# Later and closer-packed transposition of the embedding stages in a DLRM tower: stage schedule moved towards each stage's first use

## The reference

```python
e = jnp.stack([tbl_0[ids[:, 0]], ..., tbl_31[ids[:, 31]]], axis=1)    # (2048, 32, 64)
z = jnp.sum(e, axis=-1)                                               # (2048, 32)
outer = jnp.einsum('bpd,pde,bpe->bp', e[:, II], kernels, e[:, JJ])    # 496 pairs i < j
h = jnp.concatenate([z, outer, dense_ctx], axis=1)                    # 544 features
h = jnp.maximum(h @ W_top1 + b_top1, 0.0)                             # 512
h = jnp.maximum(h @ W_top2 + b_top2, 0.0)                             # 256
y = h @ W_top3                                                        # 1
```

## Time and profile before

| | |
|---|---|
| median of 3 runs | 1015.3 us (1012.37 to 1015.33) |
| the profiled execution's own time | 1018.13 us |
| its span, first to last instruction | 1016.3 us |
| PE busy | 886.5 us, 87% of the span |
| DVE busy | 641.3 us, 63% |
| POOL busy (issuing gathers) | 483.6 us, 48% |
| ACT busy | 69.3 us, 7% |
| DMA | 28.20 MB, mean 28 GB/s |

### The profile page before, as it was taken

The page is one execution under the profiler, slowest core; times in us unless marked ns, Lnnn a source line. Parts: engine busy times, 40 slices in busy tenths (PEclk is TensorE's granted clock), DMA queues, the critical chain, the costliest instruction groups (busy, mean ns, idle before and its releaser), DMA issues.

```text
span 1016.3 us, 11896 instructions
## 1 busy us (share of the span) xinstructions
PE 886.5 (87%) x4608; PEld 311.6 (31%) x4608; DVE 641.3 (63%) x579; ACT 69.3 (7%) x113; POOL 483.6 (48%) x518
## 2 busy tenths in 40 slices
PE   0323579699999999998999999998999999999998
PEld 0111123223333333333333333323333333333333
DVE  0102257578887575687877656676787657688850
ACT  0000000000000001000000101000000101000001
POOL 5774735536565444555666444554556445400000
PEclk9956779999999999999999999999999999999999
DMA  9310101101111000110111010011101000000000
GB/s 348 107 27 15 27 14 19 21 12 23 23 21 23 17 17 18 20 21 20 22 23 22 15 19 17 19 22 19 21 19 24 15 17 19 19 1 1 1 1 0
DMA packets 19777, 28.20 MB, mean 28 GB/s; under 512 B 8901, under 2 KB 9413, under 8 KB 18825
## 3 DMA queue, kind: packets, MB, share of 16 engines
q0 software_dynamic: 16384, 16.81, 8.6%
q1 hardware_dynamic: 3336, 10.63, 2.9%
HBM read 27.40 MB, written 0.01 MB: 27 GB/s over the span
## 4 chain that ended last, share of the span: by engine, by line
PE 77%; another core or an unknown queue 8%; issue 7%; DVE 4%; DMA 2%; ACT 1%; SPq 1%; POOL 1%; DVEq 0%; POOLq 0%
PE m_ps L386 39%; PE acc L398 21%; PE tr L341 4%; DVE prod L300 3%; PE tr L328 3%; PE tr L347 2%; PE m_ps L387 2%; DMA w_sb<-in_w 2%; PE m_ps L341 1%; PE tr L339 1%; PE m_ps L347 1%; PE tr L353 1%; POOL gathered L176 1%; SPq L186 1%
## 5 line engine op out<-in xcount | busy, mean ns | idle before, releaser
L300 DVE TENSOR_TENSOR prod<-m_ps,x_t 128x1024 f32<-128x1024 f32 x512 | 604.3, 1219 | 302.5 <-PE m_ps L387 180.7
L176 POOL DMA_INDIRECT gathered<-in_tbl,idx x512 | 482.9, 943 | 403.4 <-DVE prod L300 178.2
L386 PE MATMUL m_ps<-x_t,k_sb 64*128 64x512 f32 x1024 | 501.4, 623 | 74.6 <-DVE prod L300 35.6
L387 PE MATMUL m_ps<-x_t,k_sb 64*128 64x512 f32 x1024 | 502.3, 624 | 0.0
L386 PEld LDWEIGHTS m_ps<-x_t,k_sb 64*128 64x128 f32 x1024 | 180.7, 191 | 346.9 <-issue 261.6
L398 PE MATMUL acc<-prod,sel 128*32 128x512 f32 x2048 | 247.0, 600 | 0.0
L387 PEld LDWEIGHTS m_ps<-x_t,k_sb 64*128 64x128 f32 x1024 | 180.6, 191 | 0.0
L398 PEld LDWEIGHTS acc<-prod,sel 128*32 128x32 f32 x2048 | 53.7, 109 | 176.5 <-issue 119.6
L328 PE MATMUL tr<-ident,gathered 128*128 128x128 f32 x256 | 44.5, 299 | 50.6 <-DMA gathered<-in_tbl,idx 41.4
L213 ACT ACTIVATE x_t<-tr 128x512 f32<-128x512 f32 x64 | 38.2, 597 | 471.7 <-PE tr L328 275.3
L287 DVE TENSOR_REDUCE z_nat<-gathered 128x8 f32<-128x512 f32 x64 | 43.1, 675 | 38.1 <-DMA gathered<-in_tbl,idx 38.1
(11 more groups left out here) (24 smaller groups left out, 39.6 us busy)
## 6 DMA issues: line engine op xcount, KB each, us to landing
gathered<-in_tbl,idx POOLq DMA_INDIRECT x512
k_sb<-in_kmat SPq DMA_DIRECT2D x7, 1024.0 KB, 14.3
w_sb<-in_w SPq DMA_DIRECT2D x1, 1280.0 KB
k_sb<-in_kmat SPq DMA_DIRECT2D x2, 256.0 KB, 4.2
k_sb<-in_kmat SPq DMA_DIRECT2D x1, 512.0 KB, 6.4
w_sb<-in_w SPq DMA_DIRECT2D x1, 512.0 KB
idx<-in_ids SPq DMA_DIRECT2D x1, 256.0 KB, 2.7
z_sb<-in_dense_t SPq DMA_DIRECT2D x4, 32.0 KB
```

Of the source, the lines that this page charges most:

```text
L176: nc.gpsimd.indirect_dma_start(out=gathered[:, G % GR, t, f, :], out_offset=None, in_=tables[2 * (STAGES - 1 - a) + f], in_offset=bass.Ind ...
L300: nc.vector.tensor_tensor(prod[:, p % PR, :, :], m_ps[:, p % MR, :, :], other, ALU.mult).then_inc(prod_ready, 1)
L386: nc.tensor.matmul(m_ps[:, p % MR, 0, :], k_sb[0:D, d, :], x_t[0:D, q % 2, a0, :], start=True, stop=True)
L387: nc.tensor.matmul(m_ps[:, p % MR, 1, :], k_sb[D:P, d, :], x_t[D:P, q % 2, a1, :], start=True, stop=True).then_inc(unit_done, 1)
```

## The change

The table of places is redrawn and the gates move with it; no instruction is added or taken away. In quarter 0, stages 6, 7, 8 and 11 to 15 move back by 1, 1, 1, 2, 4, 5, 7 and 10 groups; stages up to 8 now stand directly ahead of the group that first uses them, later ones one group earlier. In a later quarter, stage 0 stands behind group 28 of the quarter before, stage 1 behind 30, and then stage a behind the group just ahead of its first use: 31, then 0, 1, 2, 3, 5, 7, 9, 11, 14, 17, 20, 23 of its own quarter, and 26 for stage 15. The entry "s" moves to group 28. The gates open four groups ahead of the transposition in place of three: they begin at group 24, 26, 27, 28, 29, 30, 31 of the quarter before and 1, 3, 5, 7, 10, 13, 16, 19, 22 of its own.

```diff
--- before.py
+++ after.py
@@ -61,11 +61,11 @@
 
 def group_of_stage(q, a):
 
-    return 18 + 32 * (q - 1) + 2 * a
+    return min(NG * q - 4 + 2 * a, NG * q + FIRST[a] // GROUP - 1)
 
 
 for _a in range(STAGES):
-    _g = 0 if _a < 3 else min(FIRST[_a] // GROUP - (_a > 5), (4 * _a - 7) // 3)
+    _g = FIRST[_a] // GROUP - (_a > 8)
     BEFORE.setdefault((0, _g), []).append(("x", 0, _a))
 for _q in range(1, NQ):
     for _n in range(H1 // P):
@@ -75,8 +75,8 @@
     AFTER.setdefault((_q, 13), []).append(("y", _q - 1, 0))
     for _a in range(STAGES):
         AFTER.setdefault(divmod(group_of_stage(_q, _a), NG), []).append(("x", _q, _a))
-    AFTER.setdefault((_q, 18), []).append(("s", _q, 0))
-AFTER.setdefault((0, NG - 1), []).append(("s", 0, 0))
+    AFTER.setdefault((_q, 28), []).append(("s", _q, 0))
+AFTER.setdefault((0, 28), []).insert(0, ("s", 0, 0))
 ORDER = [e for q in range(NQ) for g in range(NG) for e in BEFORE.get((q, g), []) + AFTER.get((q, g), [])]
 PLACE = {e: n for n, e in enumerate(ORDER)}
 
@@ -167,7 +167,7 @@
                     t, f = divmod(n, 2)
                     if q:
 
-                        pool.wait_ge(prod_ready, GROUP * (group_of_stage(q, a) - 3) + n)
+                        pool.wait_ge(prod_ready, GROUP * (group_of_stage(q, a) - 4) + n)
                     k = G * GATHERS + n
                     if k >= IN_FLIGHT:
```

## The result

The changed kernel takes 1140.94 us (median of 3 runs, 1137.72 to 1144.64) against 1015.3 us before: ratio 1.125, 95% interval 1.119 to 1.131. It is slower by an eighth. Its profiled execution has a span of 1139.1 us, 122.8 more than before.

The account below looks back on a forecast made before the run. PE mostly bounds the kernel, with gathers closer than about 1.5 us delaying TensorE's reports as second bound. Terms 87 - 28.2 + 3.6 - 8.3 - 8.1 + 23.2 + 16.0 + 0.9 = +86.1 us gave 1101 us, range 1035 to 1155.

Parts of the forecast that it names:

- the one with 0.50: Total time: the forecast's own band, 1070 to 1134 us, given chance 0.50.
- Term 1: Ends of quarters: packed gathers delay TensorE's signals, 29 us a boundary, +87 us for three (21 to 120).
- The price of the 15-run: Quarter 0 before the change: 15 unbroken gathers cost 10.9 us, 0.73 us each.
- the even groups of 10 + 1.8 us: Boundaries: the self-limiting run makes five groups take 10 + 1.8 us in place of 6.07, 29 us a boundary.
- Term 2: Same stretches lose their present excess, groups 8 to 24 getting fewer gathers: -28.2 us; stages 0 and 1 keep theirs, +3.6.
- Term 3: Quarter 0: the run of 16 gathers ends at 8, -8.3 us; the run of 15 goes, -8.1 us.
- Terms 4 and 5: PE waits for ScalarE's copies: just-before-use transpositions 29 x 0.80, +23.2 us; behind dense layers 18 x 0.89, +16.0; stage 0, +0.9.
- Term 6: Row sums moved on VectorE: free, since it idles at each group's end.
- Short price: Boundaries: 0.18 us per gather, 21 us in place of 87; 1035 us, band 1020 to 1070, chance 0.25.
- Heavy price: Boundaries: 1.0 us per gather, and late copies of stages 3 to 6 on PE's path; 1134 to 1194 us, chance 0.15.
- Faster: Boundaries: gates hold gathers to one per product, so boundaries cost nothing; 1011 us, chance 0.06.

Follow-up runs that it names:

- Experiment 12: The changed kernel with a GpSimd memset of 128x336 behind every gather, which puts gathers 1.51 us apart: 984.8 us, ratio 0.953.
- experiment 6: The kernel before, with only the gates of quarters 1 to 3 opened for 16 gathers of two stages at once: 1277.4 us, ratio 1.260.
- kernel 9: The kernel before with a GpSimd memset of 128x336 behind every gather, gathers 1.51 us apart: 969.2 us, ratio 0.935.
- Experiment 3: The changed kernel with stages 7 to 15 of quarters 1 to 3 transposed one group earlier, gates untouched: 1116.2 us, ratio 1.098.
- experiment 5: The changed kernel with a GpSimd memset of 128x256 behind every gather, gathers 1.44 us apart: 1053.6 us, ratio 1.039.
- experiment 1: The changed kernel with only the gates spread, opening at groups 18 to 54 counted from the quarter before: 1102.3 us, ratio 1.084.

## Why the prediction was right, and where its sizes were off

The forecast was 1101 us with a range of 1035 to 1155, and slower at 0.91; it came out at 1140.9. Mechanism and sign hold. The sum was 36.7 us short (86.1 against 122.8), by the table 15.7 of them at the boundaries, 9.5 ahead of the 28th reduction of quarter 0 and 11.7 between the boundaries; and the time lies in the band to which I gave 0.15, not in the one with 0.50.

**Term 1, the boundaries: right in kind, too small, and with the wrong picture.** It carried "The price of the 15-run gives 40 x 0.73 = 29 us a boundary" from quarter 0 to the ends of the quarters, 87 in all. Experiment 12 has the same order with the lateness nearly gone, in another round of runs. Against its boundaries those of the changed kernel are 32.1, 31.5 and 33.3 us longer, 97.0 together. POOL issues 40 gathers in each, so the price is 0.81 a gather, between my 0.73 and my upper bound of 1.0. But the even groups of 10 + 1.8 us on which I had it come out don't exist, nor does an unbroken run of 40. The gates chop it into 16, 10 and 15 in the first boundary (the 15 with two slightly longer gaps), and 16, 11 and 16 in the other two; and the groups from the 28th reduction of quarter 1 on take 22.9, 5.5, 12.5, 6.1 and 19.8 us. I had taken the self-limiting as a relief, but each piece is long enough to hold TensorE's reports to its end, and what is held lies just where PE can't go on without it: row sums, then stage 0; stage 3, then its first product. At the 10.8 us for 16 of experiment 6, 40 gathers are 27 us; the 5 or so that are left I put down to the blocked handovers in this order. That last share is worked out, not measured by itself.

**Term 2, the excess that goes away: right in the main.** Between the 1st and 28th reduction of quarters 1 and 2 the change is 5.1 and 4.2 us worse than forecast, in quarter 3 2.4. Some of it is copies still 1 us late at stages 12 and 13, where one gather follows each product as before; PE is then idle 1.6 to 1.7 us ahead of the product instead of 0.69. I had written that groups 14 to 24 would pass at 5.5 us; of each three, one takes 7.8.

**Term 3, quarter 0: wrong in its working.** I expected the run of 16 to end at 8 and the run of 15 to go. In the changed kernel there are still runs of 16 (99.5 to 119.2 and 152.3 to 172.0 us), since the slots come free in other pairs. The gain ahead of the 28th reduction was 11.1 us, 9.5 less than the terms made it. Experiment 12 shows what the table of quarter 0 is worth once lateness is out of the way: 28.8 us, by demand that comes later, which no term of mine had. No term had the longest run either, 48 gathers from 29.3 to 88.0 us in the kernel before and 46 in the changed one; beside it stand the transpositions with the latest copies of both, 16.1 and 18.5 us.

**Terms 4 and 5, the handovers: right.** The idle times on PE are 0.69 and 0.87 us against 0.80 and 0.89. In experiment 12 against 9 the change loses 45.5 us behind the 28th reduction of quarter 0; 2.9 of that are five transpositions that it moves there out of quarter 0 (0.58 each), which leaves 42.6, with 2.5 us of waits for data and some copies up to 1.3 us late in it. The terms said 40.1, less the two handovers of quarter 0 38.5. Experiment 3 gave back 14.9 us of them by one group of distance, half of what I had expected of it.

**Term 6** (the sums on VectorE are free): DVE is busy 643.8 against 641.3 us and is never the releaser that PE waits longest for. Right as far as the trace shows.

**The rivals.** Short price (1035): out. Heavy price (1134 to 1194): the time lies at its lower end, and in part by its own second reason, late copies that lie directly on PE's path. Of the stages that it named, only stage 3 was hit (2.8, 11.3 and 11.7 us late); stages 4 to 6 came 0.04 us behind, and the 14.5 us for the row sums were in no rival. The price per gather was 0.81, not 1.0. It had 0.15, and I gave the milder one 0.50 on the argument that "a slower PE closes the gates sooner"; the gates did close, and it didn't help. Faster (1011): out, a boundary costs 31 to 33 and not under 1.5.

The rule of the Trainium skill, SBUF — State Buffer, section "Who interferes with whom", that PE and ACT never wait on anyone and that DMA never contends with a compute engine, is one about ports. Read as a promise that gathers cost the compute engines nothing, it fails here: copies came up to 18.5 us late beside unbroken gathers in the changed kernel, and a change of the spacing alone brought that down to 5.2 us in experiment 5 and to 1.3 in experiment 12. That ports have a part in it is shown by no run.

## What to carry to other kernels

When GpSimd issues indirect DMAs while TensorE feeds other engines, look at the time from each transposition's end to its copy; if it swells beside unbroken gathers, put the gathers further apart, by gates that follow the work or simply by a short instruction behind each one. Here a pause that made POOL busier took 3.5 to 6.5% off an already tuned kernel, and the best spacing lay between "late signals" and "late data", so it has to be tried at two or three lengths; the longest one took only 1.3% off. And a stage is better handed through ScalarE one group before its first use: done just before, it costs 0.7 to 0.9 us each time, and it also takes away the slack that hides a late signal. Count on less than the full sum of these waits, though: in experiment 3 half of it came back.

## What the runs showed of the hardware

**The spacing, in numbers.** With gathers 1.25 us apart, copies came up to 20.6 us late (experiment 1, quarter 0) and were released some 3 us after the run ended in the two runs shown (2.9 and 3.0 us). Behind the run of 46 in the changed kernel it took longer: the last gather is through at 89.38, VectorE's next products start at 93.28 and 96.95, and ScalarE's copy at 97.03, 7.7 us after the run. At 1.44 us apart they were 0 to 8.1 late, at 1.51 us 0 to 1.3, at 1.65 us 0.05 at most (the very first stage left aside, whose copy starts 5.0 to 6.8 us late in every kernel). Each gather is 0.94 us of GpSimd and 0.30 us of gap, so the bare rate of 1.25 us is the worst one of those tried.

**It is TensorE's reports that I saw late,** to ScalarE and to VectorE. TensorE itself goes on (experiment 6: next product 0.59 us after the transposition began), and what the others report to it is not late: in experiment 6 PE has 43 idle times inside runs of ten gathers or more; 39 of them end 0.05 to 0.15 us behind an instruction of VectorE, two 0.10 and 0.14 us behind a copy on ScalarE, and two at the landing of gathers. The ends of matmuls are modelled in these traces, so whether the signal is late or the last writes that it stands for can't be told from them; nor does any run say through what the gathers act on it. That stays open.

**The kernel before is not equally fast in every round.** It took 1016.0 to 1016.7 us in two rounds and 1033.6 to 1036.6 us in two others, while the paused kernel 9 ran at 969.2 us in one of the slower ones, below the 979.0 of the nearest kernel in a faster one. That close gathers cost more in the slower rounds would explain it; I didn't test this. The record names the same chip for a round of either kind, so that it is the chip is not shown.

**Idle time costs twice.** After PE's waits of 11.9 and 14.5 us it resumed at 1.2 GHz (granted clock 0.50 from 305.36 to 310.00 and from 617.11 to 620.60 us, and 1.22 us for a matmul that takes 0.69 or 0.59), to which at least part of the 17.5 us of added PE busy time belongs.
